# Mixture-of-experts kernel: weight rows dealt to the partitions in blocks instead of in turn

## What is computed

```python
x = x + xattn(layernorm(x), ctx, Wq, bq, Wk, bk)      # attention weights made of the context
h = layernorm(x).reshape(4096, 1024)
logits = h @ gate_w.T + gate_b                        # 32 experts
topk_logits, topk_idx = top_k(logits, 4)              # each row goes to 4 experts
gate = min(h @ w_gate[e] + b_gate[e], 7)              # w_gate, w_up: 1024 x 512 for each expert
up   = clip(h @ w_up[e] + b_up[e], -7, 7)
act  = (up + 1) * gate * sigmoid(1.702 * gate)
x    = x + sum over the 4 experts of weight * (act @ w_down[e] + b_down[e])   # w_down: 512 x 1024
```

## Time and profile before

| | us |
|---|---|
| median of 3 runs (3279.0 to 3282.75) | 3280.85 |
| the profiled execution | 3284.01 |
| its span, first to last instruction | 3282.2 |
| TensorE busy | 3120.8 (95%) |
| VectorE busy | 1720.9 (52%) |
| ScalarE busy | 1280.6 (39%) |
| GpSimd busy | 595.1 (18%) |

### The profile page before, as it was taken

One profiled execution on the slowest core, in us unless ns is written; L12 is line 12 of the kernel. 1 busy time (PEld: TensorE's weight loads), 2 busy tenths in 40 slices (PEclk: granted clock), 3 DMA queues, 4 the chain that ended last, 5 costly groups with the idle time before them and its releaser, 6 DMA issues.

```text
span 3282.2 us, 46620 instructions
## 1 busy us (share of the span) xinstructions
PE 3120.8 (95%) x15456; PEld 1609.9 (49%) x15457; DVE 1720.9 (52%) x2851; ACT 1280.6 (39%) x1299; POOL 595.1 (18%) x502
## 2 busy tenths in 40 slices
PE   6799899995999999999999999999999999999997
PEld 3455555553455444455455444544555445455553
DVE  4576767774453544554544545444455444454432
ACT  3553434422342434443433434344344333343421
POOL 0023323322111111111111111111111111111111
PEclk8899999997999999999999999999999999999999
DMA  4123222354564555556555655655565655555432
GB/s 149 64 104 124 103 84 104 104 166 146 144 171 117 148 154 154 174 159 198 155 155 150 173 154 166 192 173 144 142 171 164 197 156 153 154 163 144 110 63 58
DMA packets 210439, 468.03 MB, mean 143 GB/s; under 512 B 57761, under 2 KB 57761, under 8 KB 210114
## 3 DMA queue, kind: packets, MB, share of 16 engines
q1 hardware_dynamic: 164514, 314.84, 27.2%
q0 software_dynamic: 45856, 152.33, 22.2%
HBM read 354.64 MB, written 112.46 MB: 142 GB/s over the span
## 4 chain that ended last, share of the span: by engine, by line
PE 71%; DMA 3%; SPq 1%; issue 1%; ACT 0%; DVE 0%; POOL 0%; ACTq 0%; POOLq 0%; DVEq 0%
PE psG L1167 22%; PE psU L1167 22%; PE psY L1189 22%; PE psX L1173 4%; PE psA L1180 2%; DMA bias<-in_L_ffn_b_down 2%; DMA idxg<-slots 0%; SPq L959 0%; DMA idxs<-slots 0%; SPq L112 0%; DMA acc<-y,idxs 0%; SPq L962 0%; DMA xg<-xn_tab,idxg 0%; ACT aT L1057 0%; DVE gt L1122 0%
## 5 line engine op out<-in xcount | busy, mean ns | idle before, releaser
L1189 PE MATMUL psY<-W,aT 128*128 128x512 f16 x3456 | 777.9, 382 | 23.1 <-ACT aT L1057 23.1
L1167 PE MATMUL psG<-W,xT 128*128 128x512 f16 x3456 | 772.4, 380 | 2.9 <-ACT xT L1053 2.9
L1167 PE MATMUL psU<-W,xT 128*128 128x512 f16 x3456 | 769.4, 379 | 0.0
L1167 PEld LDWEIGHTS psG<-W,xT 128*128 128x128 f16 x3456 | 338.8, 98 | 413.0 <-issue 6.1
L1189 PEld LDWEIGHTS psY<-W,aT 128*128 128x128 f16 x3456 | 339.7, 98 | 406.2 <-ACT aT L1057 24.5
L1167 PEld LDWEIGHTS psU<-W,xT 128*128 128x128 f16 x3456 | 338.2, 98 | 375.6
L1114 DVE SCALAR_TENSOR_TENSOR y<-bias,idxs,y 128x1024 f32<-128x1024 f32 x144 | 185.0, 1284 | 544.7 <-ACT y L1064 544.7
L123 DVE SCALAR_TENSOR_TENSOR W<-stage,W 128x2048 f16<-128x2048 f32 x192 | 438.7, 2285 | 4.8 <-ACT W L118 4.8
L1021 POOL DMA_INDIRECT acc<-y,idxs x144 | 227.4, 1579 | 1011.9 <-DVE y L1114 996.3
L1064 ACT ACTIVATE y<-psY,idxs 128x1024 f32<-128x1024 f32 x144 | 160.5, 1114 | 604.6 <-DMA idxs<-slots 577.9
L118 ACT ACTIVATE W<-stage 128x2048 f16<-128x2048 f32 x192 | 365.1, 1902 | 10.8 <-issue 5.5
(11 more groups left out here) (136 smaller groups left out, 2305.1 us busy)
## 6 DMA issues: line engine op xcount, KB each, us to landing
stage<-in_L_ffn_w_gate SPq DMA_DIRECT2D x64, 1024.0 KB
stage<-in_L_ffn_w_up SPq DMA_DIRECT2D x64, 1024.0 KB
stage<-in_L_ffn_w_down SPq DMA_DIRECT2D x64, 1024.0 KB
stage<-in_x SPq DMA_DIRECT2D x32, 512.0 KB
xr<-in_x SPq DMA_DIRECT2D x32, 512.0 KB
acc<-xr SPq DMA_DIRECT2D x32, 512.0 KB
xn_tab<-x2h SPq DMA_DIRECT2D x32, 512.0 KB
bias<-in_L_ffn_b_down SPq DMA_DIRECT2D x32, 512.0 KB, 13.6
```

The source lines that it names most:

```text
L1167: op = pe.matmul(ps[:], xT[:, k, :, a], weights(par, c, offset + k * I, I), start=k == 0 and n == 0, stop=k == KH - 1 and n == 2)
L1189: op = pe.matmul(psY[:, h * HALF:(h + 1) * HALF], aT[:, k, :, a], weights(par, c, 2 * KH * I + k * H + h * HALF, HALF), start=k == 0 and n ...
```

## The change

Row `8p + k` (w_gate, w_up) or `4p + k` (w_down) now lies on partition p as its k-th row. A chunk is then one contiguous run of 8 KB for each partition: half of the 16 KB that the partition's rows of one matrix take in DRAM. The columns of the rows in `xn_tab` and of `ahl` have to be in the matching order, so that block k of a transpose holds columns k, 8 + k, 16 + k, ... (k, 4 + k, ... for `ahl`). For that the four writes into `x2h` and `ahl` go through a view of three dimensions: the source is read in order, and each element is written 128 pairs (512 bytes) behind the one before, eight times (four for `ahl`), then the write goes back to the next pair. The LO writes read their HI operand in the same order. The number of instructions, their sizes and every wait stay as they were.

```diff
-        w_dram = [w.rearrange("e (k p) n -> e p k n", p=P) for w in (w_gate, w_up, w_down)]
+        w_dram = [w.rearrange("e (p k) n -> e p k n", p=P) for w in (w_gate, w_up, w_down)]
...
+        x2h_cols = [x2h[:, j, :, :].rearrange("p (k q) a -> p q k a", k=KH) for j in range(2)]
+        xs2_cols = xs2[:, :].rearrange("p (q k) -> p q k", k=KH)
...
-                    act.activation(x2h[:, n % 2, :, HI], xs2[:], ACT.Copy, scale=S_ROWS).then_inc(s_hi2, 1)
+                    act.activation(x2h_cols[n % 2][:, :, :, HI], xs2_cols, ACT.Copy, scale=S_ROWS).then_inc(s_hi2, 1)
...
-                    dve.scalar_tensor_tensor(out=x2h[:, n % 2, :, LO], in0=xs2[:], scalar=S_ROWS, in1=x2h[:, n % 2, :, HI],
+                    dve.scalar_tensor_tensor(out=x2h_cols[n % 2][:, :, :, LO], in0=xs2_cols, scalar=S_ROWS,
+                                             in1=x2h_cols[n % 2][:, :, :, HI],
                                              op0=ALU.mult, op1=ALU.subtract).then_inc(s_lo2, 1)
...
+        ahl_cols = ahl[:, :, :].rearrange("p (k q) a -> p q k a", k=KI)
+        av_cols = av[:, :].rearrange("p (q k) -> p q k", k=KI)
...
-                act.activation(ahl[:, :, HI], av[:], ACT.Copy, scale=S_ACT).then_inc(s_ahi, 1)
+                act.activation(ahl_cols[:, :, :, HI], av_cols, ACT.Copy, scale=S_ACT).then_inc(s_ahi, 1)
...
-                dve.scalar_tensor_tensor(out=ahl[:, :, LO], in0=av[:], scalar=S_ACT, in1=ahl[:, :, HI],
+                dve.scalar_tensor_tensor(out=ahl_cols[:, :, :, LO], in0=av_cols, scalar=S_ACT, in1=ahl_cols[:, :, :, HI],
                                          op0=ALU.mult, op1=ALU.subtract).then_inc(s_alo, 1)
```

## The result

The changed kernel takes 3460.25 us in the median against 3280.43 (with a fourth execution of the kernel before), a ratio of 1.0547 with a 95% interval of 1.0529 to 1.0566. The profiled execution took 3459.93 us (span 3458.2, 176.0 more than before).

The account below looks back on a forecast made before the run. TensorE, 95% busy, was taken to bound the kernel, with ScalarE's x2h write in the attention step's loop. 3284.0 + 18.3 (attention block) - 7 (weight loads) = 3295.3 us profiled, 3292 median; range 3268 to 3321.

Parts of the forecast that it names:

- the four holes: Experts: four VectorE waits for a bias load, 46.8 us together; TensorE's down product then waits 20.8 us.
- psR's wait for x2T: Attention block: TensorE waits for ScalarE's x2T copy before psR; forecast to stay near 0.9 us a step.
- The price of a hop: The four writes: 1.85 ns an element on VectorE; x2h LO +0.67 us, x2h HI +0.55 us, each 0 to +1.4.
- The statement of the upper end: Bound on the hopping write: the same surcharge once for operand HI and once for the target, 2.6 ns an element.
- The attention block's sum: Attention block: x2h HI 11.6 us, x2h LO 5.9, last batch's steps 0.8, together +18.3 us; bounds 0 to +50.
- the forecast's own rule: Attention block: 21 steps pay ScalarE's surcharge whole; VectorE's is paid where idle time ahead of `xr` doesn't cover it.
- the seven without cover: Seven of 24 two-batch steps with no VectorE idle time ahead of `xr`: each pays the full 0.67, together 4.7 us.
- the four with little: Four two-batch steps with 0.24 to 0.53 us of idle time ahead of `xr`: pay what is left, together 1.2 us.
- the steps that were to absorb them: Two-batch steps outside the 21: TensorE has no idle time ahead of psR and absorbs ScalarE's surcharge.
- ahl covered: Experts, 144 tiles: 6.2 us of cover from the gate product hides the slower ahl writes, so they cost nothing.
- The weight loads: Weight queue: 57,344 packets vanish; biases land 0.75 us sooner at four boundaries; gain 7 us, bounds 0 to 29.
- Rival 2, the hop is dear: Attention block: the loop pays +50 us less 7, giving 3324 us; chance 0.13.

Follow-up runs that it names:

- e3_hop_scalar_only: Against the changed kernel, VectorE's LO write into x2h is in order again, ScalarE's HI write keeps its hops: 3420.35 us (1.0421).
- e8_bias_early: Against the kernel before, the next expert's three bias loads are issued ahead of the third tile's weight chunks: 3252.81 us (0.9912).
- e7_warm_filler: Against the changed kernel, TensorE makes 24 extra products of 256 columns ahead of its wait for x2T in each two-batch step: 3455.11 us (1.0532).
- e6_hop_in_read: Against the changed kernel, the four views' loops are swapped, so writes go in order and the source is read with hops: 3313.23 us (1.0094).
- e5_prices: The kernel before with a block of single 1024-element writes and reads at various hops ahead of it: 3437.58 us, the first 154 for the measurements.
- e2_down_blocks_only: Against the changed kernel, only w_down stays in blocks and only ahl is written with hops; x2h is written in order: 3280.54 us (1.0001).

## Why the prediction was wrong

- **What bounds the kernel**: right in part. ScalarE's x2h write is on the way of a step (e3_hop_scalar_only), and the expert block was full but for the four holes, as e8_bias_early shows. But the forecast had psR's wait for x2T stay near 0.9 us "as the loop stretches with it"; it went to 4.13 us, and TensorE's granted clock behind it fell to 0.50. And with both writes hopping, VectorE's chain closes about half of the two-batch steps (no idle time ahead of `xr` in 12 of 22), and a restored clock gave back only 5 us (e7_warm_filler, where it is 19 of 22).
- **The price of a hop: here the forecast failed.** It took 1.85 ns an element from a float32 read and put the end of its bounds at 2.6. Measured are 4.46 ns. The read price was right for reads (e6_hop_in_read, 2051 ns for a forecast 2055); what was wrong was to price a narrow write by a wide read. With the rule of e5_prices, the trace of before had a better row. The forecast noted that x2h HI "already pays for its 4-byte steps", 1354 ns instead of 1060, and passed over it. That is 4 x (1354 - 209)/1024 = 4.5 ns for every 16 bytes, and the hopping write touches 16 bytes for every element. The statement of the upper end, a surcharge once for each port, had no row under it.
- **The attention block's sum: its rule failed too.** 18.3 us were forecast, 180.5 measured. With the measured prices (+3.42, +3.34) the forecast's own rule gives 21 x 3.42 = 72 for ScalarE. VectorE pays in the two-batch steps 23 for the seven without cover, 12 for the four with little and 19 for the twelve whose slack of 1.1 to 3.7 us no longer covers it. The last batch pays 8 x 2.8 = 23. That is 149 in all, so by the rule the price explains 131 of the missing 162. That it comes so near is partly luck, for its parts are off. In the two-batch steps ScalarE's hops alone cost 112 and not 72: the steps that were to absorb them wait as well, and TensorE works slowly behind each hole. VectorE's alone cost 50 (forecast's rule: 54), but on top of ScalarE's only 19, and both together 131. In the last batch VectorE's LO write waits for the HI write, so that both surcharges are on its way, 5.1 us a step (41.1/8) instead of 2.8. ScalarE's `ah` write is recorded with a median of 1662 ns instead of 1480; that goes with ScalarE's own hopping write ahead of it (1643 with ScalarE's hops alone, 1444 with VectorE's), and whether it costs time is open.
- **ahl covered**: right, at 3.4 us a tile where 0.8 were forecast (e2_down_blocks_only).
- **The weight loads**: 57,344 packets fewer, right. The gain at the holes was forecast at 7 us; the four waits together went from 46.8 to 44.4 us, the expert block is 4.3 us shorter (2.2 to 4.3 over five traces). The last bias of the four boundaries still landed 13.0 to 13.7 us after its issue, against 13.3 to 13.9. The direction is right, and the size 3 to 5 us too large.
- **The clock**: the forecast had none in the attention block. With ScalarE's hops alone it costs up to 57 us by the sum above, which no run tested by itself; with both all but 5 us of it is hidden behind VectorE (e7_warm_filler).
- **Rival 2, the hop is dear**, was the one that happened, at 4.46 ns instead of the 2.6 that it allowed. The two figures that the forecast set beside it from the Trainium skill, 1.71 and 2.50 ns ("Vector Engine (DVE) Microarchitecture Reference", section Measured stream behaviour on trn2), are measured there on 4-byte words; for those ScalarE's float32 write here (1.93 us, 1.68 ns an element) agrees with the first. The kernel's writes are of 2 bytes, so neither figure was theirs. The chances of the forecast's dearer side add up to 0.67, not 0.66.

## What to carry to other kernels

On ScalarE and in VectorE's two-source form, a permutation that is put into a write of 2-byte elements was paid at 4.4 ns each time the write moved to another 16 bytes; put into the read of the same writes, it cost 1.7 to 1.85 ns an element, and in TensorE's transposes some 50 ns a weight load, mostly covered. An instruction that already runs slower than its in-order rate tells what the next wider step may cost: divide its time, less its fixed part, by the 16-byte stretches that it touches before widening the step. And where a small load stands behind large ones in a queue, its place was worth more (26 us) than the size of the large ones' pieces (about 4).

## What was not expected of the hardware

- Float16 writes 4, 8 and 16 bytes apart take 1.33, 2.44 and 4.68 us for 1024 elements on ScalarE, and then hardly more up to 4096 bytes (4.47 to 4.76); float32 writes 1.92 to 2.04 from 32 bytes on, and pairs of them in order 1.08 with hops of 512 bytes from pair to pair.
- VectorE's one-source form pays less for the same hop: 2.73 us at 512 bytes, with 0.74 at 4 bytes, against 4.70 for the two-source form.
- TensorE's clock in the attention block followed its idle time within a step: behind the hole of 4.13 us shown above psR ran at 1.2 GHz, and in e7_warm_filler, with filler work in the hole, the same psR ran at 2.4 GHz (the stretch of psR):

```profile
443.80:445.50 1.70, 1.70 (x16) 1.70 (x17) 1.67 (x5) 0.00 (x0) 0.00 (x0) 1.00 0.00 0
```
